# A four-layer graph network: fp16 row parts turned by transposing DMAs, later turns, and four row buffers in the attention layers

## What is computed

```
x = layernorm(x + GIN(x))    # z = x + sum of neighbours; relu(z @ W1 + b1) @ W2 + b2
x = layernorm(x + SAGE(x))   # mean_agg @ Wl.T + b + x @ Wr.T; batch norm; relu; + x
x = layernorm(x + GAT(x))    # relu(gat_conv), relu(gat_conv) at width 1024, then h @ Wfc + bfc
x = layernorm(x + GCN(x))    # normalised sum, @ W.T, batch norm, gelu, + x
```

## Time and profile before

| | us |
|---|---|
| median of 3 runs (4434.73 to 4446.85) | 4443.02 |
| the profiled execution | 4436.53 |
| its span, first to last instruction | 4435.0 |
| PE busy in the span | 3705.9 (84%) |
| DVE, ACT, POOL busy | 1952.9, 1477.9, 1445.9 |
| mean granted TensorE clock | 0.916 of full speed |

### The profile page before, as it was taken

One profiled execution on the slowest core, in us unless ns is written; L12 is line 12 of the kernel. 1 busy time (PEld: TensorE's weight loads), 2 busy tenths in 40 slices (PEclk: granted clock), 3 DMA queues, 4 the chain that ended last, 5 costly groups with the idle time before them and its releaser, 6 DMA issues. The chain is left out here.

```text
span 4435.0 us, 61816 instructions
## 1 busy us (share of the span) xinstructions
PE 3705.9 (84%) x21000; PEld 2265.5 (51%) x21000; DVE 1952.9 (44%) x4003; ACT 1477.9 (33%) x2671; POOL 1445.9 (33%) x1268
## 2 busy tenths in 40 slices
PE   4599993699997999884999999998678888669832
PEld 3144441355545666663677767666544444234432
DVE  7166666333324444275211111105655555147677
ACT  1333332222223344353333333323333333323332
POOL 2444433332102222253232322214345545323111
PEclk6799996799998999997999999999889999979955
DMA  1734437543424555496444343417756666567588
GB/s 63 223 117 142 142 114 247 163 141 117 140 85 176 210 212 195 163 272 206 139 134 146 126 150 133 140 65 211 220 209 222 215 210 215 176 196 238 190 287 278
DMA packets 306106, 778.90 MB, mean 176 GB/s; under 512 B 39814, under 2 KB 39814, under 8 KB 303952
## 3 DMA queue, kind: packets, MB, share of 16 engines
q1 hardware_dynamic: 238800, 556.39, 35.3%
q0 software_dynamic: 67200, 221.25, 17.3%
HBM read 491.80 MB, written 284.56 MB: 175 GB/s over the span
## 5 line engine op out<-in xcount | busy, mean ns | idle before, releaser
L320 PE MATMUL bank<-w_hi,t_r_lo 128*128 128x344 f16 (+1 forms) x2560 | 843.1, 329 | 0.0
L321 PE MATMUL bank<-w_lo,t_r_hi 128*128 128x344 f16 (+1 forms) x2560 | 841.6, 329 | 0.0
L322 PE MATMUL bank<-w_hi,t_r_hi 128*128 128x344 f16 (+1 forms) x2560 | 841.0, 329 | 0.0
L2247 DVE SCALAR_TENSOR_TENSOR t_z<-t_h,t_z 128x256 f32<-128x256 f32 x640 | 334.9, 586 | 888.7 <-DMA t_h<-h 870.0
L2216 POOL TENSOR_TENSOR t_r_lo<-t_r,t_r_hi 128x512 f16<-128x512 f32 x320 | 375.2, 1176 | 664.9 <-ACT t_r_hi L2284 659.8
L320 PE MATMUL bank<-l_z_hi,w_lo 128*128 128x512 f16 x960 | 364.8, 380 | 1.5 <-DVE l_z_lo L1764 1.5
L321 PE MATMUL bank<-l_z_lo,w_hi 128*128 128x512 f16 x960 | 364.8, 380 | 0.0
L322 PE MATMUL bank<-l_z_hi,w_hi 128*128 128x512 f16 x960 | 364.5, 380 | 0.0
L2281 ACT ACTIVATE t_r<-bank,vec_scaled 128x512 f32<-128x512 f32 x320 | 219.7, 686 | 428.0 <-PE bank L2312 323.4
L322 PEld LDWEIGHTS bank<-w_hi,t_r_hi 128*128 128x128 f16 x2560 | 251.8, 98 | 172.1 <-issue 7.5
L321 PEld LDWEIGHTS bank<-w_lo,t_r_hi 128*128 128x128 f16 x2560 | 252.2, 98 | 159.8 <-issue 5.2
(11 more groups left out here) (268 smaller groups left out, 6541.9 us busy)
## 6 DMA issues: line engine op xcount, KB each, us to landing
t_h<-h SPq DMA_DIRECT2D x160, 512.0 KB, 4.3
h<-b_wide SPq DMA_DIRECT2D x80, 516.0 KB, 2.9
h<-w_hi SPq DMA_DIRECT2D x80, 516.0 KB, 2.9
sum_gat<-a_out SPq DMA_DIRECT2D x80, 514.0 KB
l_x<-x SPq DMA_DIRECT2D x40, 1024.0 KB, 9.0
h<-l_h SPq DMA_DIRECT2D x40, 1024.0 KB, 5.8
b_h<-h SPq DMA_DIRECT2D x40, 1024.0 KB, 6.7
b_x<-x SPq DMA_DIRECT2D x40, 1024.0 KB, 9.1
```

The lines of the kernel that those rows point to most:

```text
L320: pe.matmul(out, s_lo, m_hi, start=(k == 0), stop=False)
L321: pe.matmul(out, s_hi, m_lo, start=False, stop=False)
L322: mm = pe.matmul(out, s_hi, m_hi, start=False, stop=last)
L2247: ins = v.scalar_tensor_tensor(out=z[u][:, s, cols], in0=hrow[s % 2][:, cols], scalar=z[u][:, s, HC + h:HC + h + 1], in1=z[u][:, s, cols], ...
```

## The change

**GIN.** The rows are split before they are turned. ACT writes `row_hi` and DVE `row_lo` (fp16, nodes on the partitions) from `z` in SBUF, subtile by subtile, between the steps for the hidden layer of the group before. SP then issues two transposing DMAs for each group, 128x2048 fp16 each, into `z_hi[u]` and `z_lo[u]`, which lie in weight space that isn't in use yet. PE's 320 fp32 transposes go, and the two banks they used serve the hidden layer, which has four now. The bias is added into `y` and not into `x`.

**Batch norm of SAGE.** `turn_back` and the high parts are cut in two halves of two chunks, with a third of a product after the first half and another before the second.

**Attention layers.** `hrow` has four buffers, in dead weight space (`w_lo`), and each row load waits only for the combine of the same subtile of the group before. POOL issues the gathers of a group ahead of the `norm.pool` that they stood behind. In the second layer, SP's store of a group comes after the row loads of a later one, and the load of `x` behind the store that it depends on.

```diff
@@ gin_stage
-    z_hi = kn.buffer(mem, "g_z_hi", [P, 4, D], F16)
-    z_lo = kn.buffer(mem, "g_z_lo", [P, 4, D], F16)
+    row_hi = kn.buffer(mem, "g_row_hi", [P, S, D], F16)
+    row_lo = kn.buffer(mem, "g_row_lo", [P, S, D], F16)
+    z_hi = [kn.spare(False, u * 4 * S * P * 2, [P, S * 4, P], F16) for u in range(2)]
+    z_lo = [kn.spare(True, u * 4 * S * P * 2, [P, S * 4, P], F16) for u in range(2)]
-    tp = [kn.bank[0], kn.bank[1]]
-    mid_ps = [kn.bank[6], kn.bank[7]]
+    mid_ps = [kn.bank[n] for n in (0, 1, 6, 7)]
...
+        def turn(g):
+            i, u = divmod(g, 2)
+            sp.wait_ge(mid.sem, mid.at(max(g - 1, 0) * 4))
+            sp.wait_ge(hi_done.sem, hi_done.at(g * S + S))
+            sp.dma_start(z_hi[u], row_hi[:].rearrange("p s c -> p (s c)"),
+                         transpose=True).then_inc(turned_in[u].sem, 16)
+            sp.wait_ge(lo_done.sem, lo_done.at(g * S + S))
+            sp.dma_start(z_lo[u], row_lo[:].rearrange("p s c -> p (s c)"),
+                         transpose=True).then_inc(turned_in[u].sem, 16)
...
+        load_x(0)
+        load_x(1)
+        turn(0)
         for g in range(G):
-            if g + 1 < G:
-                load_x(*divmod(g + 1, 2))
+            if g + 2 < G:
+                load_x(g + 2)
             if g:
                 store(g - 1)
+            if g + 1 < G:
+                turn(g + 1)
@@ vector
             for m in range(4):
+                if not last:
+                    add_sums(*following(i, u), m)
                 dve.wait_ge(r_hi_done.sem, r_hi_done.at(g * 4 + m + 1))
                 v.tensor_tensor(r_lo[:, m, :], r_f[m % 2][:], r_hi[:, m, :], ALU.subtract).then_inc(r_lo_done.sem, 1)
-            if not last:
-                add_sums(*following(i, u))
+                if not last:
+                    low_part(*following(i, u), m)
@@ tensor
+            pe.wait_ge(turned_in[u].sem, turned_in[u].at(i * 32 + 32))
             for m in range(4):
 
-                pe.wait_ge(r_done.sem, r_done.at(g * 4 + (m - 1 if m >= 2 else 0)))
-                split_product(pe, mid_ps[m % 2][:],
+                pe.wait_ge(r_done.sem, r_done.at((g - 1) * 4 + m + 1))
+                split_product(pe, mid_ps[m][:].rearrange("p (s n) -> p s n", s=S),
...
             for s in range(S):
-                if s >= 2 and not last:
-                    turn(*following(i, u), (2 * s - 4, 2 * s - 3))
@@ batch_norm_stage, tensor
             products(i, u, 1)
-            products(i, u, 2)
+            products(i, u, 2, (0, 1))
             if not last:
-                turn_back(*following(i, u))
-            products(i, u, 3)
+                turn_back(*following(i, u), (0, 1))
+            products(i, u, 2, (2,))
+            products(i, u, 3, (0,))
+            if not last:
+                turn_back(*following(i, u), (2, 3))
+            products(i, u, 3, (1, 2))
@@ gat_stage
-    hrow = two("t_h", [P, HC], F32)
+    hrow = kn.w_lo[:, 0:S * 2 * HC].bitcast(F32).rearrange("p (s c) -> p s c", s=S)
...
+    def load_rows(sp, g, s):
+
+        if g:
+            i, u = divmod(g - 1, 2)
+            sp.wait_ge(z_ready[u].sem, z_ready[u].at(i * S + s + 1))
+        sp.dma_start(hrow[:, s, :], h_dram[g * GROUP + s * P:g * GROUP + (s + 1) * P, LOGITS:]).then_inc(h_in[s].sem, 16)
...
         low_parts(0, 0, range(CH))
+        load_sums(2)
         for g in range(G):
-            if g + 2 < G:
-                load_sums(g + 2)
             if g + 1 < G:
                 low_parts(*divmod(g + 1, 2), range(CH))
+            if g + 3 < G:
+                load_sums(g + 3)
             if not first:
                 norm.pool(pool, *divmod(g, 2))
```

## The result

The changed kernel takes 4291.4 us (4288.64 to 4296.51, 4 runs) against 4440.9 (4434.73 to 4446.85, 4 runs) beside it: ratio 0.9665, 95% interval 0.9648 to 0.9682. That is 149.5 us less; the forecast was 4298.

| stage | before | after | gain | forecast |
|---|---|---|---|---|
| GIN | 486.9 | 462.0 | 24.9 | 19 |
| batch norm, SAGE | 547.9 | 522.3 | 25.6 | 19 |
| first attention layer | 953.3 | 943.7 | 9.6 | 15 |
| second attention layer | 616.8 | 527.2 | 89.6 | 92 |

The account below looks back on a forecast made before the run. PE was taken to bound all four stages. GIN -19, batch norm -19, attention starts -15 and -8, second attention layer -84 make -145 from 4436.5: 4291.5, plus 6.5 for the runs' median, 4298; range 4245 to 4440.

Parts of the forecast that it names:

- GIN, what goes: GIN stage: PE loses the 16 fp32 turns of a group, 1.74 us, so 22.86 becomes 21.1 us.
- What is added: GIN stage: DVE's pace of 2.1 us a subtile makes PE wait 0.4 us more, so a group takes 21.5 us.
- The transposing DMAs: GIN stage: the pair takes 8.6 us at most, from bounds of 3.0 and 26.9, and is just hidden in 8.5.
- The price by bytes and landing time of ordinary loads: GIN stage: a transposing pair priced as two 512 KB row loads, 4.3 us each from issue to landing, 8.6 us.
- the price by the piece: GIN rival: each 256-byte piece costs a packet's 0.105 us, 26.9 us a pair, 4666 us in all; chance 0.14.
- late by some us: GIN rival: pairs of 9 to 15.5 us make PE wait and go cold; 12 us gives 4368; chance 0.19.
- Batch norm: Batch norm stage: turns in halves remove PE's 19.1 us wait for DVE to empty a bank, -19 us.
- The start of the attention layers: Both attention layers: rows asked for at once, bytes at 355 GB/s set the first matmul; -15 us first layer, -8 second.
- a combine and the split: First attention layer's start: work between the last bytes at 2087 and the first matmul at about 2091.5.
- The second attention layer: Second attention layer: rows asked for a group ahead end DVE's waits; 24.2 us a group, 482 in all, -84 us.
- DVE's 0.8 us to spare: Second attention layer: DVE's last combine of a group ends 0.8 us before PE wants it at 24.2 us.

## Why the prediction was right

The forecast of 4298 was 6.6 us above the median, well inside its range; the sum made against the profiled execution, 4291.5, stands beside an execution of 4288.6. The mechanism held in each stage. The closeness of the total is in part luck: GIN and batch norm gained 5.9 and 6.6 us more than their terms, the attention layers 5.4 and 2.4 less, and these errors partly cancel.

*GIN, what goes* was right: groups take 21.11 and 21.18 us in turn, so 1.7 of the 22.86 went. *What is added*: the 0.4 us more for the last `r_lo` did not come. My step by step gave DVE a pace of 2.1 us a subtile; it was 2.0 (254.90, 256.90, 258.89 in its timeline), and the relu, the cast and the high part fitted between. 19 times 0.4 is 7.6 us, and the stage is 5.9 us better than the sum.

*The transposing DMAs* were the step on which all hung, and I chose 8.6 us a pair from a range of ninefold; nothing in the trace of before could decide it, and that the choice came out was luck as much as reading. It was 7.0. The price by bytes and landing time of ordinary loads was the right side; the price by the piece made the pair four times too long, because a piece of 256 bytes cost 0.022 us and not the 0.105 of an average packet. The two runs with more DMAs show that the room was small: a pair slower by 1.5 us would have begun to cost, as the rival "late by some us" said, and by more than its wait where PE fell to the lower clock. The figure of 1309 ns for each 128x128 block, from the page VectorE: DVE Perf Modes of the Trainium skill (The three transpose paths), does not add up over blocks here: 16 of them landed in 4.5 to 4.7 us. The 261 GB/s of the Trainium skill's page DMA: Bandwidth & Descriptors (Latency and other measured facts), which the page states for a non-contiguous middle dimension, gave an estimate of 2.0 us a DMA; one more in the queue cost 2.3 to 2.5.

*Batch norm*: the mechanism was right, the size was not, because I took the sum of the idle times (19.1) for the loss. The distances of the starts give 26, the run with the part put back 25.3.

*The start of the attention layers*: the bytes were not the limit that I took them for. In the first layer the second group's combine began 17.6 us after the first load and ran through without a wait for rows, where I had the last row at 23.7. The term was mis-sized at the combine: I allowed some 4.5 us after the last row for "a combine and the split", and 16 combines at 0.87 us came instead, nine of them held by POOL's low parts. The trace of before had the sign, at the same place:

```profile
2089.76 8.41 DVE L2247 SCALAR_TENSOR_TENSOR t_z<-t_h,t_z 128x256 f32<-128x256 f32 x8 [5.79 <-DMA t_h<-h]
```

The first layer gained 9.6 us and not 15; in the second layer the rows of group 1 also stood behind two loads of `x` on SP, and the first matmul came 38.0 us after the first row load where I had 33.6.

*The second attention layer*: right. From the first product to the last are 479.5 us (482 in the sum, 565.6 before), and PE has no gap between 3240 and 3620. DVE's 0.8 us to spare held, though its combines went from 615 to 645 ns and its norm from 575 to 1121.

## What to carry to other kernels

A transposing DMA of fp16 tiles takes PE's turns off its path when it lands between the last cast and the next product; only the stage's start pays. Count the room from issue to landing pair by pair and not from two medians, and reckon with the clock as well as the wait if it is short. When two loads end a wait one behind the other, their gains don't add: here the gathers alone brought 4 us, the row buffers alone 52, both 94. Ask of each what the other will still hold. Take what a gap costs from the distances of starts, since idle time is counted from a modelled end.

## What was not expected of the hardware

- A combine or a norm of DVE (both operands of the combine in SBUF, fp32) that starts inside a `t_r_lo` of POOL ends 0.28 us after it, 1.38 us long in place of 0.47 and 0.54. DVE's moments (L1425, 0.69 us) and its sums that read a PSUM bank (L2274, 0.68 us, three cases) take the same time inside a `t_r_lo` and alone. Which operand makes the difference was not tested by a run.
- A transposing DMA of 128x2048 fp16 holds SP's queue for 1.7 to 3.1 us at its issue, where an ordinary DMA of this queue takes 0.43 us (median, 0.71 or less in nine of ten); eight of 128x512 for the first group took 1.25 to 1.32 each, 10.5 us together for the same 1 MB (211.74 to 222.21).
- After PE waits of 3.1 to 4.2 us the following matmuls started 0.43 us apart in 15 of 19 groups and 0.216 in four; after waits of 0.7 to 1.1 us always 0.216.
